# Segment-end picks with eight copies of their 13 columns, issued behind the count products of both superbatches of a slot

## The reference: what is computed

```
def _L0_gnn_ref(z, edge_weight, edge_src, edge_dst, Wm, bm, W1, b1, W2, b2):
    Wd, Ws, ww = (Wm[:H], Wm[H:2 * H], Wm[2 * H])
    msgs = z[edge_dst] @ Wd + z[edge_src] @ Ws + edge_weight[:, None] * ww[None, :] + bm
    agg = jax.ops.segment_max(msgs, edge_dst, num_segments=n)
...
    agg = jnp.where(deg[:, None] > 0, agg, jnp.zeros((), dtype=z.dtype))
    W1a, W1b = (W1[:H], W1[H:])
    hidden = jax.nn.relu(z @ W1a + agg @ W1b + b1)
    return hidden @ W2 + b2
...
def _sage_conv(x, src, dst, Wl, bl, Wr, n_nodes):
    msg = x[src]
    agg = jax.ops.segment_sum(msg, dst, num_segments=n_nodes)
...
    mean = agg / jnp.maximum(deg, 1.0)[:, None]
    return mean @ Wl.T + bl + x @ Wr.T
...
h = jax.nn.relu(_sage_conv(x, src, dst, W1l, b1l, W1r, n))   # _L1_gnn_ref, in short
out = _sage_conv(h, src, dst, W2l, b2l, W2r, n)
...
x = _layernorm(x + _L0_gnn_ref(...))
x = _layernorm(x + _L1_gnn_ref(...))
```

## Time and profile before

| what | value |
|---|---|
| median of 3 runs | 1476.27 us (1471.65 to 1479.07) |
| the profiled execution's own time | 1471.77 us |
| its span, first to last instruction | 1469.7 us |
| granted PE clock over the span | 0.740 of full speed |
| busy share: PE, PEld, DVE, POOL, ACT | 81%, 60%, 58%, 53%, 28% |

### The profile page before, as it was taken

How to read it: one execution, slowest core, us unless ns; L and a number is a source line. 1 busy time by engine, 2 the same in 40 slices (tenths; PEclk the granted TensorE clock), 3 DMA queues, 4 the chain that set the end, 5 groups by cost and what they waited for, 6 DMA issues and landing times.

```text
span 1469.7 us, 24820 instructions
## 1 busy us (share of the span) xinstructions
PE 1183.3 (81%) x6646; PEld 883.2 (60%) x6677; DVE 847.4 (58%) x3070; ACT 408.5 (28%) x1248; POOL 775.9 (53%) x828
## 2 busy tenths in 40 slices
PE   3798877988697887668798878878769678889998
PEld 3566656766575664556465666555556455665676
DVE  4455556665556655655655656566565555564455
ACT  2222222222222222222222222223222222221365
POOL 4555565665566556655665655565655555500132
PEclk8655566556758767866868567779668878899999
DMA  6322232223223323322332323332334322434521
GB/s 148 97 62 59 67 73 64 71 76 77 72 71 66 86 70 88 68 72 75 83 88 66 75 67 95 81 85 67 71 75 105 87 68 64 112 92 115 151 58 46
DMA packets 118181, 118.04 MB, mean 80 GB/s; under 512 B 23463, under 2 KB 102659, under 8 KB 118035
## 3 DMA queue, kind: packets, MB, share of 16 engines
q1 hardware_dynamic: 91110, 64.18, 17.2%
q0 software_dynamic: 24864, 50.97, 14.7%
q10 hardware_dynamic: 2061, 1.20, 0.3%
HBM read 103.60 MB, written 12.68 MB: 79 GB/s over the span
## 4 chain that ended last, share of the span: by engine, by line
PE 53%; another core or an unknown queue 19%; issue 10%; DVE 7%; ACT 4%; SPq 3%; DMA 3%; ACTq 2%; DVEq 0%
PE bank L1536 12%; PE bank L1539 8%; PE bank L1523 6%; PE bank L1718 5%; PE bank L1482 5%; PE bank L1587 4%; PE bank L1555 3%; PE bank L1470 3%; ACT area L789 2%; DVE area L1090 2%; DVE area L1110 2%; PE bank L1542 2%; ACTq L774 1%; DVE area L1091 1%
## 5 line engine op out<-in xcount | busy, mean ns | idle before, releaser
L924 POOL DMA_INDIRECT area<-zs_d,area x757 | 726.7, 960 | 512.9 <-PE bank L1482 201.3
L1110 DVE TENSOR_TENSOR_SCAN area<-area,bank 128x512 f32<-128x512 bf16 x196 | 249.9, 1275 | 395.1 <-PE bank L1482 225.6
L1536 PE MATMUL bank<-area 128*128 128x13 f32 x1564 | 306.5, 310 | 197.6 <-ACT area L789 148.9
L1536 PEld LDWEIGHTS bank<-area 128*128 128x128 f32 x1564 | 293.5, 263 | 244.0 <-ACT area L789 170.3
L781 ACT CAST adj_w<-bank 128x325 f32 x391 | 175.6, 449 | 858.2 <-PE bank L1542 451.8
L1090 DVE TENSOR_SCALAR area<-area 128x128 bf16<-128x128 f16 x782 | 216.1, 276 | 110.7 <-remote 83.6
L1091 DVE TENSOR_SCALAR area<-area 128x325 bf16<-128x325 f16 x782 | 248.0, 317 | 0.0
L1539 PE MATMUL bank<-area 128*128 128x325 bf16 x782 | 227.1, 383 | 0.3 <-issue 0.3
L1523 PE MATMUL bank<-ident,area 128*128 128x128 f32 x782 | 174.1, 364 | 0.0
L1482 PE MATMUL bank<-ident,area 128*128 128x128 f32 x762 | 160.4, 346 | 0.0
L1587 PE MATMUL bank<-adj_w,area 128*128 128x512 bf16 (+4 forms) x494 | 119.3, 384 | 28.9 <-DVE area L1122 9.2
(11 more groups left out here) (166 smaller groups left out, 1002.9 us busy)
## 6 DMA issues: line engine op xcount, KB each, us to landing
area<-mask_d SPq DMA_DIRECT2D x195, 128.0 KB
area<-zs_d,area POOLq DMA_INDIRECT x757
area<-zs_d SPq DMA_DIRECT2D x640, 0.5 KB
area<-wp_d SPq DMA_DIRECT2D x585, 3.0 KB
area<-parts_d SPq DMA_DIRECT2D x20, 384.0 KB, 7.8
zr_d<-area SPq DMA_DIRECT2D x24, 128.0 KB
area<-zr_d SPq DMA_DIRECT2D x6, 512.0 KB, 3.9
area<-scale_d SPq DMA_DIRECT2D x11, 256.0 KB, 4.1
```

The source lines that it names most:

```text
L924: pool.indirect_dma_start(gring[:, g % GR * 4 + s % 2 * 2 + u, :], None, x if g < RAW else zs_d[0:N, :], bass.IndirectOffsetOnAxis(ap=src_ ...
L1110: nc.vector.tensor_tensor_scan(S[:, g % 2, 0:n], mask[:, g % MR, 0:n], T_BANK[g % 2][:, 0:n], S[:, (g + 1) % 2, 511:512] if g else 0.0, AL ...
L1536: nc.tensor.matmul(o[:, 384:384 + W], St[:, b * P:(b + 1) * P], sel[:, g % 2, u, s % 2, :], start=u == 0, stop=u == 1)
```

## The change

The loop over a group's two superbatches is cut in two. The first loop has the count products of both superbatches, each behind `made` and `ae_sb`. Only then come the waits for `st_sb` and `picked`, and a second loop with the picks of both. A pick reads `sel` through a view that repeats its 13 columns 8 times (`WIDE`), so it streams 104 columns and writes 104 columns of the bank, 384 to 487. ACT still reads the first 13. `ae_ps` is incremented behind the picks of each superbatch.

```
--- before.py
+++ after.py
+WIDE = 8
...
                 def adjacent(g):
-                    pe.wait_ge(st_sb, g + 1)
-                    pe.wait_ge(picked, g + 1)
                     for s in supers(g):
                         o, r, q = A_BANK[s % 2], s % HR, (s - 1) % HR
                         pe.wait_ge(made, s + 1)
                         if s >= 2:
                             pe.wait_ge(ae_sb, s - 1)
                         for u in range(2):
-                            b = s % 2 * 2 + u
-                            nc.tensor.matmul(o[:, 384:384 + W], St[:, b * P:(b + 1) * P], sel[:, g % 2, u, s % 2, :],
-                                             start=u == 0, stop=u == 1)
-                        for u in range(2):
                             last = nc.tensor.matmul(o[:, 0:COLS], hot_l[:, r, u, :], hot_d[:, r, u, :], start=u == 0,
                                                     stop=u == 1 and s == 0)
                         if s:
                             last = nc.tensor.matmul(o[:, 0:COLS].rearrange("p (h w) -> p h w", w=W)[:, :, 0], hot_l[:, q, 1, :],
                                                     hot_x[:, q, 0:NT], start=False, stop=True)
+                    pe.wait_ge(st_sb, g + 1)
+                    pe.wait_ge(picked, g + 1)
+                    for s in supers(g):
+                        o = A_BANK[s % 2]
+                        for u in range(2):
+                            b = s % 2 * 2 + u
+                            last = nc.tensor.matmul(o[:, 384:384 + WIDE * W].rearrange("p (n w) -> p n w", w=W), St[:, b * P:(b + 1) * P],
+                                                    sel[:, g % 2, u, s % 2, :].unsqueeze(1).broadcast_to([P, WIDE, W]),
+                                                    start=u == 0, stop=u == 1)
                         last.then_inc(ae_ps, 1)
```

## The result

The changed kernel took 1436.11 us (median of 4 runs, 1428.65 to 1450.27) against 1476.97 us for the kernel before on the same chip: a ratio of 0.9712, 95% interval 0.9663 to 0.976, so 2.9% faster. The forecast was 1447 us, in a range of 1395 to 1484.

What follows compares the result with a forecast made beforehand. No engine was full; PE was busiest at 81%, its signals reaching other engines late. 1471.8 us + 0 (picks) - 29 (order) + 0 (signals) + 0 (clock) = 1442.8, with 4.5 for the median 1447; range 1395 to 1484.

Steps and rivals of the forecast that it cites:

- Wider picks cost nothing: PE's picks: a pass has a floor that 104 columns do not exceed, so widening from 13 was taken as 0 us.
- the prediction's own sign: PE's picks in the changed profile: four passes still 0.45 us at full clock and 0.86 at half; longer means width costs.
- the 16 us that was named as the most: PE's picks: upper bound on the wider passes' cost if the half-clock rows' difference were all the columns'.
- the 250 us: PE's picks: upper bound if the broadcast view of `sel` cost the whole floor once more per pass; taken as 0.
- Order: PE's 65 waits for `st_sb`: count products run inside them, saving 0 to 57 us; the middle, 29 us, was taken.
- the 50 us forecast: PE's wait for line 789, ACT's copy to `St`: to stand fewer times or shorter than 198 us by about 50.
- Clock counted as 0: PE's granted clock: whether it rises was left open and 0 us counted, since slots pass alike at either clock.
- The far rival: PE's share of the chain: clock rises to 0.86 and saves 109 us; chance 0.17 for anything below 1418 us.
- Signals: First superbatch's `ae_ps` to ACT comes one count group later, 0.30 or 0.57 us; counted as 0 in the sum.
- slower rival: ACT's copies come late and delay `St` by 0.30 us in 98 slots, 29 us, 1505; chance 0.16 above 1484.
- Nothing reaches the end: Rival: PE's late signals set the slots' pace, saved time reappears at the next wait; about 1475 us, chance 0.20.
- Scans to between 16 and 17 in 100 us: DVE's scans, which count slots, were to rise from 16 in 100 us to between 16 and 17.

Runs made afterwards that it cites:

- e11: The changed kernel timed again, unchanged, on a chip with late PE signals: 1417.82 us, ratio 0.9695 to the kernel before.
- e10: The kernel before with only the picks widened to 104 columns, old order, late PE signals: 1440.11 us, ratio 0.9859 to the kernel before.
- e9: The changed kernel with picks of 13 columns, so new order only, late PE signals: 1440.02 us, ratio 0.9837 to the kernel before.
- e3: The changed kernel with each superbatch's picks directly behind its own count products, prompt PE signals: 1171.57 us, ratio 0.9978 to the kernel before.
- e8: The kernel before with wider picks only, old order, and half of POOL's gathers: 1026.12 us, against 1083.78 for the kernel before with half the gathers.

## Why the prediction was right

**The forecast's size.** The sum was -29 us, from the order alone; measured is -41 us (1476.97 - 1436.11), in e11 -44. The way and the place were right, and one term, the clock, was put at nothing. That the time fell near the middle of the range owes something to the order term, whose size was a guess between 0 and 57.

**Wider picks cost nothing**: nearly right. The step took 0.11 and 0.21 us a pass from the earlier trace rows, and all passes but the first of a string still take that. By the prediction's own sign (0.45 and 0.86 us for four passes, "if longer, the width costs") the width does cost: 0.06 us a string at full clock and 0.10 at half (e10). The changed kernel has one string of eight a slot, with medians of 0.957 and 1.810 us against 0.893 and 1.706 in e9: an estimated 15 us of PE's time over 195 slots with two thirds of them at full clock. About half of it comes back at the transposes right behind, which start closer to each other. This is the 16 us that was named as the most; the 250 us are excluded. The clock's saving below is what is left after it.

**Order**: right in its mechanism, as far as the traces tell, and lucky in its size. 57 us at most, and 29 taken as the middle because no row divided it; e9 has 24 us (17 to 31 by its interval). PE's wait for line 789 went from 198 us to 7 in the changed kernel, by more than the 50 us forecast, because most of it moved: 106 us now stand at the first count product, behind line 783, as was named. All idle time ahead of `adjacent` fell by 36 us in e9 and by 50 in the changed kernel, which fits count products that run inside the wait. e3, which was to take one superbatch's count products out of it, fell on the prompt chip, so this part of the cause is argued and not shown.

**Clock counted as 0**: the term that was mis-sized. It is 21 us (14 to 27 by e10's interval), the cost of the wider picks already taken off. The earlier trace rows were read as a clock of which little reaches the end, since slots at 0.60 and 0.77 pass at the same pace. But the stretches at high clock were those with more work on PE, the pieces of layer 1, as the prediction itself said. A comparison of stretches that differ in work can't price the clock. The far rival, 109 us less if the clock rises to 0.86, was wrong by a factor of five too: PE's busy time did fall, from 1183 us to 1091 in e10, but some 70 of those 92 us came back as idle time ahead of `adjacent` (270 us, from 198). Where PE is the limit and its signals are prompt, the same width saved 58 us (e8), all that PE's busy time fell by.

**What the clock follows.** Width alone moved the mean clock from about 0.74 to 0.836 (e10) while the long waits between bursts stayed. The Trainium skill, page "TensorE: Matmul & The Clock Gate", section "HAM oscillation — how this bites in real kernels", names such waits as what puts the clock back; waits alone don't account for e10, which has more of them (270 us ahead of `adjacent`) and the higher clock. The same page, section "What's actually happening", says that the clock follows how busy PE has been. The trace can't say whether that holds here, since it is left open what counts as busy: the passes of e9 and e10 are as many and, but for the first of a string, as far apart (median start to start 0.112 us at full clock and 0.213 at half in both), and their columns are what differs, 13 and 104.

**Signals, slower rival**: its sign came and its cost did not. ACT's second copy of line 781 now starts within 0.25 us of the first copy of 782 in 132 of 195 slots (71 before). But e9, which has the late first `ae_ps` without the width, is 1.6% faster where the rival had 29 us more. Whether a smaller cost hides in it is not known: e3, which was to measure it directly, fell on the prompt chip and tells nothing of it. **Nothing reaches the end** holds in one condition only: on the prompt chip, where POOL sets the pace.

**Scans to between 16 and 17 in 100 us**: not seen. The changed kernel's full stretches have 15 or 16, and 41 us over twelve hundred are below what a count by 100 us can show.

## What to carry to other kernels

Put the products that need only old data ahead of the wait for fresh data, whenever the engine arrives at that wait early. They can pay at most what they take, and less where the wait shows up again under another name: 24 us of 57 here. Where a narrow matmul starts the next one no sooner than a wide one does, more columns are nearly free (0.06 to 0.10 us a string of passes here), and they can raise the granted clock; price that by changing the columns alone, not by comparing stretches of one trace that carry different work. And time both kernels on the same chip: the pace of the whole loop here was POOL's gathers on one chip and PE's late signals on others, and a change that gave 3% on the second has halves that gave 0.4% at most on the first.

## What the runs showed of the hardware

PE's semaphore updates were recorded up to 6 us after the matmul that gives them, in all profiles with the full gathers where the kernel before takes 1462 to 1477 us, and never over 0.2 us late in the four profiles of the chip where it takes 1174, with the same programs. The two times are a fifth apart. With half of POOL's gathers the late signals nearly vanish on a late chip (9 us in sum against 233); without SP's single-row loads they stay (302). So they go with the gathers, or with the pace at which all of it runs; what delays them, and why one chip is free of it, stays open and was not tried further.
